# Value parts of an attention kernel: VectorE's subtraction replaced by a whole copy on ScalarE and a third step on GpSimd

## The reference

```python
edge = _attn(lin(x, n2e_q), lin(x, n2e_k), lin(x, n2e_v), adj.transpose(0, 2, 1))
edge = _ln(edge + x, norm1_g, norm1_b)
node = _attn(lin(x, e2n_q), lin(edge, e2n_k), lin(edge, e2n_v), adj)
node = _ln(x + node, norm2_g, norm2_b)
h = gelu(lin(node, ffn_w1, ffn_b1))
out = _layernorm(x + _ln(node + lin(h, ffn_w2, ffn_b2), norm3_g, norm3_b))
```

## Time and profile before

| | |
|---|---|
| median of 3 runs | 2962.13 us (2961.11 to 2962.54) |
| profiled execution, its own time | 2963.18 us |
| its span, mean granted clock | 2961.0 us, 0.989 |
| PE, DVE, ACT, POOL busy | 97%, 59%, 52%, 44% |
| attention passes | about the first 1600 us |

### The profile page before, as it was taken

One profiled execution on the slowest core, in us unless ns is written; L12 is line 12 of the kernel. 1 busy time (PEld: TensorE's weight loads), 2 busy tenths in 40 slices (PEclk: granted clock), 3 DMA queues, 4 the chain that ended last, 5 costly groups with the idle time before them and its releaser, 6 DMA issues.

```text
span 2961.0 us, 55170 instructions
## 1 busy us (share of the span) xinstructions
PE 2870.9 (97%) x17920; PEld 2400.4 (81%) x17920; DVE 1761.4 (59%) x5914; ACT 1549.1 (52%) x4138; POOL 1289.6 (44%) x1227
## 2 busy tenths in 40 slices
PE   8999999999999999999979999999999999999996
PEld 7888887888788888888868888888888888888885
DVE  7888888888888888888863332233332323333334
ACT  6777777777787877887854222222222222222221
POOL 3443534344365554546512344344343334434334
PEclk9999999999999999999989999999999999999998
DMA  6544444444566666657663011111101111110111
GB/s 197 120 112 126 117 110 116 117 123 111 147 154 162 171 170 156 166 150 176 168 155 121 22 43 58 50 57 57 57 9 55 53 53 57 57 41 22 57 36 64
DMA packets 488664, 295.44 MB, mean 100 GB/s; under 512 B 279584, under 2 KB 410784, under 8 KB 488480
## 3 DMA queue, kind: packets, MB, share of 16 engines
q1 hardware_dynamic: 488480, 293.49, 37.3%
HBM read 159.21 MB, written 67.11 MB: 76 GB/s over the span
## 4 chain that ended last, share of the span: by engine, by line
PE 81%; DVE 8%; issue 5%; ACT 4%; POOL 1%; DMA 1%; DVEq 0%; SPq 0%; ACTq 0%; POOLq 0%
PE proj L871 25%; PE proj L1335 23%; PE score L1349 12%; PE proj L1349 12%; PE score L920 5%; PE att_out L855 4%; ACT att_probs L521 2%; PE att_turn L837 2%; DVE normed L698 2%; DVE att_p_lo L769 1%; ACT turned L480 1%; DVE att_q_lo L749 1%; DVE att_stats L703 1%; DVE att_k_lo L744 1%; ACT att_p_hi L528 1%
## 5 line engine op out<-in xcount | busy, mean ns | idle before, releaser
L1279 DVE TENSOR_TENSOR hidden_lo<-hidden,hidden_hi 128x512 fp32r<-128x512 f32 x256 | 201.4, 787 | 943.1 <-ACT hidden_hi L1114 943.1
L1121 ACT ACTIVATE hidden<-proj,ffn_bias 128x512 f32<-128x512 f32 x256 | 176.6, 690 | 996.7 <-PE proj L1335 996.7
L521 ACT ACTIVATE att_probs<-att_probs,att_minus_max 128x128 f32<-128x128 f32 x1024 | 397.1, 390 | 154.7 <-DVE att_minus_max L760 154.7
L101 POOL TENSOR_TENSOR pool_scratch<-pool_scratch 128x1 f32<-128x1 f32 x144 | 38.0, 264 | 703.2 <-DVE ffn_moments L1223 402.6
L769 DVE TENSOR_TENSOR att_p_lo<-att_probs,att_p_hi 128x512 f16<-128x512 f32 x256 | 231.2, 942 | 149.2 <-ACT att_p_hi L528 149.2
L760 DVE CUSTOM_DVE_ANT_0 att_probs<-score,att_mask 128x128 f32<-128x128 f32 x1024 | 226.4, 285 | 19.2 <-PE score L920 10.7
L871 PE MATMUL proj<-weight_v_hi,source_hi 128*128 128x512 f32 x512 | 215.5, 421 | 13.7 <-DVE weight_v_lo L719 11.0
L480 ACT ACTIVATE turned<-att_turn,att_shift,att_gain 128x128 f32<-128x128 f32 x512 | 192.9, 458 | 65.6 <-PE att_turn L837 65.6
L637 POOL TENSOR_TENSOR source_lo<-source_raw,source_hi 128x512 fp32r<-128x512 f32 x128 | 163.1, 1296 | 129.6 <-ACT source_hi L544 129.6
L871 PE MATMUL proj<-source_hi,weight_k_hi 128*128 128x512 f32 x512 | 203.5, 397 | 2.3 <-DVE weight_k_lo L719 2.3
L871 PE MATMUL proj<-source_lo,weight_k_hi 128*128 128x512 f32 x512 | 203.0, 396 | 0.0
(11 more groups left out here) (157 smaller groups left out, 8520.9 us busy)
## 6 DMA issues: line engine op xcount, KB each, us to landing
att_tokens<-in_x SPq DMA_DIRECT2D x128, 256.0 KB, 3.1
source_raw<-in_x_t SPq DMA_DIRECT2D x16, 1024.0 KB, 5.5
edges_t<-turned SPq DMA_DIRECT2D x64, 256.0 KB, 2.5
source_raw<-edges_t SPq DMA_DIRECT2D x16, 1024.0 KB, 5.6
att_query_raw<-in_x_t SPq DMA_DIRECT2D x16, 1024.0 KB, 6.8
nodes_t<-turned SPq DMA_DIRECT2D x64, 256.0 KB, 2.8
source_raw<-nodes_t SPq DMA_DIRECT2D x16, 1024.0 KB, 7.5
normed<-nodes SPq DMA_DIRECT2D x16, 1024.0 KB, 5.6
```

Source lines behind the costliest of these rows:

```text
L521: nc.scalar.activation(probs[:, j, :], probs[:, j, :], ACT.Exp, bias=minus_max[:, j:j + 1], scale=-1.0, accum_out=row_sum[:, side, j:j + 1 ...
L1121: nc.scalar.activation(hidden[:, c % 2, :], up_bank[c % 2][:], ACT.Gelu, bias=bias_1[:, c:c + 1]).then_inc(activated, 1)
L1279: nc.vector.tensor_tensor(hidden_lo[:, c % 2, :], hidden[:, c % 2, :], hidden_hi[:, c % 2, :].bitcast(F32), ALU.subtract).then_inc(hidden_ ...
```

## The change

`value_high` on ScalarE now copies the bank whole, in f32, into a half of `v_rest`, after a wait that the value parts of two graphs before are done. `value_rest` on VectorE is gone. `value_low` on GpSimd casts the high part from it, subtracts it in place, casts the middle part and subtracts for the low part, with a wait between each step and the next. Value banks are now released by ScalarE, key and query banks still by VectorE, so the waits of `project` name one of two semaphores.

```diff
         def value_high(g, parity, b):
             n = value_place(g, b)
             act.wait_ge(projected, n + 1)
-            nc.scalar.copy(v_part[parity][0][:, b, :], value_bank(g, b)[:]).then_inc(proj_hi_ready, 1)
+            wait(act, values_ready, GB * g + b - 1)
+            nc.scalar.copy(v_rest[:, b % 2, :], value_bank(g, b)[:]).then_inc(proj_hi_ready, 1)
...
         def value_low(g, parity, b):
 
-            pool_gate(pool, proj_split, value_place(g, b) + 1, pool_scratch)
-            nc.gpsimd.tensor_copy(v_part[parity][1][:, b, :], v_rest[:, b % 2, :]).then_inc(v_middle_ready, 1)
+            pool_gate(pool, proj_hi_ready, value_place(g, b) + 1, pool_scratch)
+            rest = v_rest[:, b % 2, :]
+            high, middle, low = (part[:, b, :] for part in v_part[parity])
+            nc.gpsimd.tensor_copy(high, rest).then_inc(v_high_ready, 1)
+            pool.wait_ge(v_high_ready, GB * g + b + 1)
+            nc.gpsimd.tensor_tensor(rest, rest, high, ALU.subtract).then_inc(v_rest_ready, 1)
+            pool_gate(pool, v_rest_ready, GB * g + b + 1, pool_scratch)
+            nc.gpsimd.tensor_copy(middle, rest).then_inc(v_middle_ready, 1)
             pool.wait_ge(v_middle_ready, GB * g + b + 1)
-            nc.gpsimd.tensor_tensor(v_part[parity][2][:, b, :], v_rest[:, b % 2, :], v_part[parity][1][:, b, :],
-                                    ALU.subtract).then_inc(values_ready, 1)
+            nc.gpsimd.tensor_tensor(low, rest, middle, ALU.subtract).then_inc(values_ready, 1)
...
-        def value_rest(g, parity, b):
-            dve.wait_ge(proj_hi_ready, value_place(g, b) + 1)
-
-            wait(dve, values_ready, GB * g + b - 1)
-            nc.vector.tensor_tensor(v_rest[:, b % 2, :], value_bank(g, b)[:], v_part[parity][0][:, b, :],
-                                    ALU.subtract).then_inc(proj_split, 1)
-
...
-        def project(place, bank, products, chunks=range(C)):
+        def project(bank_free, bank, products, chunks=range(C)):
 
             if chunks[0] == 0:
 
-                wait(pe, proj_split, place - PROJ_BANKS + 1)
+                wait(pe, *bank_free)
...
+            if b == 2 and starts(g):
+                bank_free = (proj_hi_ready, value_place(0, 0) + 1)
+            elif b >= 2:
+                bank_free = (proj_split, split_count(g, b - 2, 1) - 2)
+            else:
+                bank_free = (proj_split, 0 if starts(g) else split_count(g - 1, b + 2, 1) - 2)
...
```

More of the change, by code:

```diff
@@ L67, in skipped, with split_count @@
     return 1 if isinstance(g, int) and g == 2 * NG - 1 and u == C - 1 else 0
+def split_count(g, u, queries):
+    return 2 * C * g + 2 * u + queries + 1
 def value_place(g, b):
@@ L320, in attention_passes @@
     projected, proj_hi_ready, proj_split = sem("projected"), sem("proj_hi_ready"), sem("proj_split")
+    v_high_ready, v_rest_ready = sem("v_high_ready"), sem("v_rest_ready")
     v_middle_ready, values_ready = sem("v_middle_ready"), sem("values_ready")
@@ L790, in body @@
                 first = starts(g) and u == 0
[L791 to L794, removed]
+                if not first:
                     mask_and_maximum(n, g if u == 1 else None)
@@ L800, in body @@
                     nc.vector.tensor_scalar(mask[:], adj[:], 0.0, MASKED, ALU.is_le, ALU.mult).then_inc(mask_ready, 1)
[L801 to L806, removed]
                 if u == 2 and not starts(g):
@@ L883, in values @@
                     pe.wait_ge(weight_lo, 3 * C * own + c + 1)
-                project(value_place(g, b), value_bank(g, b), lambda c: parts([s[:, c, b * P:(b + 1) * P] for s in x],
+                project(bank_free, value_bank(g, b), lambda c: parts([s[:, c, b * P:(b + 1) * P] for s in x],
                                                                           [w[:, c, :] for w in (wh["v"], wl["v"])]), range(c, c + 1))
@@ L892, in keys @@
             x = [s[parity] for s in (source_hi, source_lo)]
-            project(key_place(g, u) + skipped(g, u), key_bank(u), lambda c: parts([w[:, c, u * P:(u + 1) * P] for w in (wh["k"], wl["k"])],
+            project((proj_hi_ready, key_place(g, u) + skipped(g, u) - PROJ_BANKS + 1), key_bank(u), lambda c: parts([w[:, c, u * P:(u + 1) * P] for w in (wh["k"], wl["k"])],
                                                                   [s[:, c, :] for s in x]))
@@ L903, in queries @@
             x = (query_hi, query_lo) if own == 1 else [s[parity] for s in (source_hi, source_lo)]
-            project(query_place(g, u) + skipped(g, u), query_bank(u), lambda c: parts([w[:, c, u * P:(u + 1) * P] for w in (wh["q"], wl["q"])],
+            project((proj_split, split_count(g, u, 0) - 2), query_bank(u), lambda c: parts([w[:, c, u * P:(u + 1) * P] for w in (wh["q"], wl["q"])],
                                                                       [s[:, c, :] for s in x]))
@@ L913, in scores @@
             if h == 0:
-                pe.wait_ge(proj_split, query_place(g, u) + 1)
+                pe.wait_ge(proj_split, split_count(g, u, 1))
             for i in range(2):
@@ L976, in attention_passes @@
         "early_tokens_stored": (tokens_out, 16 * (NG - 1)),
-        "banks_free": ((proj_split, PROJ * last_group), (masked, UNIT * C * last_group)),
+        "banks_free": ((proj_split, 2 * C * last_group), (proj_hi_ready, PROJ * last_group), (masked, UNIT * C * last_group)),
         "residual_biased": (biased, GB * last_group),
```

## The result

The changed kernel takes 3009.1 us (median of 4 runs, 3008.0 to 3012.1) where the one before takes 2962.0 (2961.1 to 2962.5): a ratio of 1.0161, with a 95% interval of 1.0148 to 1.0175. It is slower by 47 us; 38 had been forecast, and the range of 2966 to 3030 holds it. In the profiled executions the span went from 2961.0 to 3006.2 us, 45.2 more, and this is the difference to be explained.

A forecast was written before the change was run, and what follows sets the result against it. TensorE, busy for 97% of the span, was taken to bound the kernel. Waits at the weighing, less score waits won back, plus 3.4 us of clock, came to 37.7 us on 2962.1: 3000 us (+1.3%), range 2966 to 3030.

The forecast's parts named there:

- wait at the weighing, added: TensorE's weighing in both passes: waits longer for GpSimd's value parts, 43.7 us more in all.
- wait at the scores: TensorE's scores: first pass's waits for low queries at loop returns go, 10.9 us off, 1.5 left.
- half clock: TensorE's granted clock: slow stretches behind long waits cost 10.2 us in place of 6.8, so 3.4 more.
- The longer chain: GpSimd's value part in the third unit: 4.7 us, between 4.0 and 5.2; ordinary first-pass groups wait 0.9 us each.
- the sign of an error: Weighing's wait below 10 us in total, from an f32 subtraction much cheaper than 1.2 us or an earlier inverse spread.
- First pass, behind a return: Five loop returns: weighing waits 1.9 us each, 9.5 in all; scores keep 5 x 0.3.
- The backlog of the second pass: GpSimd behind the query split: inverse spread 1.3 us late, so the weighing waits 2.4 us in an ordinary group.
- The scores of the second pass: Score waits at the second pass's loop returns: 2.7 us stay, as GpSimd is busy with a backlog.
- The clock: Half of twelve long second-pass waits followed by half clock, 6 x 1.7 = 10.2 us, in place of four now, 6.8.
- Slow clock throughout: Rival: half clock behind all the long waits, 3015 to 3034 us; chance 0.27, shared with a held ScalarE.
- Relief wins: Rival: GpSimd's chain ends before the weighing needs it, score waits go: 2937 to 2955 us; chance 0.12.
- ScalarE held by the buffer: Rival: late GpSimd stalls ScalarE's copy and the softmax, 3040 us and up; inside the slow tail, shared chance 0.27.

The follow-up runs named there:

- run 3: Kernel before, with the new way in both passes for three value parts of each group, not the one in front of the weighing: 2963.4 us, 1.0006.
- run 6: Kernel before, with the new way in the first pass only, for three value parts of four, not the one in front of the weighing: 2948.7 us, 0.9957.
- run 7: Changed kernel, with ScalarE also writing the high part from the bank, so GpSimd has three instructions per value part, not four: 2952.2 us, 0.9973.
- run 10: Changed kernel, with 95 more already met waits at the start of ScalarE's program: 3006.0 us, 1.0153.
- run 1: Changed kernel, but ScalarE also writes the high part and GpSimd makes only two parts, without the f32 subtraction (values sum wrongly): 2934.6 us, 0.9908.
- run 9: Changed kernel, with 31 more already met waits at the start of ScalarE's program: 3022.1 us, 1.0207.
- run 4: Changed kernel, with GpSimd making the value part in front of the weighing before the inverse spread, not behind it: 3018.2 us, 1.019.
- run 5: Changed kernel, with the second pass's load of the next queries issued behind a group's first transposes of the probabilities, not before: 3011.0 us, 1.017.
- run 11: Kernel before; first pass: ScalarE writes high part and whole value, GpSimd three steps; second: VectorE's last value subtraction ahead of third unit's maxima: 2971.3 us, 1.0033.

## Why the prediction was right, and where it was not

Side, size and first mechanism hold: the weighing waits for GpSimd in both passes, longest in the second, and the first pass's score waits are gone. But the terms of the sum met 45 us in another way than they had made 38:

| term, us | forecast | measured |
|---|---|---|
| wait at the weighing, added | 43.7 | 32.7 |
| wait at the scores | -9.4 | 0.0 |
| half clock | +3.4 | +11.9 |
| turns, key weights | 0 | -1.9 and +2.3 |

**The longer chain** was mis-sized. I took 4.7 us; the rows above run from the gate at 1244.78 to 1247.80 + 1.21 = 1249.01, 4.2 us. I had argued that the centring covers about half of the chain and holds GpSimd back. It is the other way round: GpSimd starts at 1244.78, VectorE at 1244.85, and the four centrings take 4.44 us where the earlier trace rows had 3.06, while GpSimd's instructions keep their length. Taken one by one the centrings last 0.96, 1.38, 0.96 and 1.37 us, and each ends 0.28 us behind one of GpSimd's casts or subtractions; the first two of the kernel before took 0.54 us each. That the one which issues first keeps the other out is also what the Trainium skill says (SBUF — State Buffer, "Who interferes with whom"); the trace agrees, with 1.38 us more on VectorE. I had used the rule for the wrong side. With 4.2 us the seven ordinary groups of the first pass lose no wait that the list shows, where 0.9 each, 6.3 us, had been summed. What had been named as the sign of an error, a cheaper f32 subtraction, is not the cause: it takes 1.17 to 1.23 us.

**First pass, behind a return:** 1.9 forecast, 10.0 / 5 = 2.0 measured; scores 1.5 left forecast, none measured. The 10.9 us that the prediction took off for the first pass hold the 0.7 where the passes meet. From 100 to 740 us the scores gained 10.2 and the weighing lost 10.0 - 0.9 = 9.1, so that the two waits together gained 1.1 us, without the clock.

**The backlog of the second pass** was right in kind and too small: the inverse spread is 2.0 us late, not 1.3. Two additional microseconds per value part had been counted; but a part whose cast lies beside VectorE's low probabilities is longer: the cast takes 1.08 instead of 0.61 and the gate 0.52 instead of 0.19. The two errors, chain and lateness, nearly cancel: 2.4 forecast for the wait in an ordinary group, 2.75 measured. Runs 3 and 6 show the backlog without the longer chain, with ScalarE's pause mixed in, and run 7 shows it gone.

**The scores of the second pass** were the step that failed. I left 2.7 us there as unchanged; it is 12.9, by ScalarE's pause. It delays the weighing's demand as well: 25.3 us at the weighing, against 29.6 in run 10 without the pause. That is why the waits behind a return, forecast at 0.9 + 1.3 = 2.2 each, came out at 0.3 to 1.9; in run 10 they are 1.9 to 2.0. That the total came so near is in part luck: 11 us less at the weighing stand against 9.4 more at the scores and 8.5 more of half clock.

**The clock** was under-counted, and not where it had been forecast. Six falls in the second pass in place of the four of the first had been summed, and the second pass has six, of 3.4 us each. Left out were three more in the first pass, from 322, 418 and 513 us on, and 3.4 us more in each of the two stretches where the passes meet: 5 x 3.4 / 2 = 8.5 us, the difference between 3.4 and 11.9. Which long wait is followed by one, and which isn't, I still can't say: in the first pass three of the five waits of 2.0 us are, and behind the wait of 2.75 us at 1249.28 none follows within 30 us.

**The rivals.** Slow clock throughout (3015 to 3034) did not come: 13 stretches, and some at the ends of the passes, for 27 waits (21 at the weighing and 6 at the scores). Relief wins: run 1 shows its full size, 27 us, and its condition, a chain without the added 2 us. ScalarE held by the buffer: not seen; its list has no wait for the value parts. GpSimd's busy time came at +229 for a forecast of +256, VectorE's at -53 for -88: over the whole span the centrings took 137.7 us where they had taken 103.0, and the low parts of the probabilities 210.8 where they had taken 231.2. The other 20 us are not traced to a line.

**Open:** what the pause is. The runs show that it comes with the loop's return, in the second pass's code, that it changes from nothing to 4 us when only the places of ScalarE's instructions change (runs 9, 10), that it shrinks when only GpSimd's order changes (run 4), and that the load of the queries has no part in it (run 5). That ScalarE's instructions arrive late is my reading. The packets of the instruction queue, which land 1.2 to 1.4 us before the end of each pause, speak for it; that they hold ScalarE's instructions, and why they come late, no run shows. Part of run 11's time is this pause, and run 7, like run 1, is without it, so run 7's 57 us is not the price of a cast alone.

## What to carry to other kernels

Taking work from an engine with slack to another with slack is paid for at the place where the receiving engine's order meets the critical one: here 2 us on GpSimd in front of a product that TensorE awaits cost 71 to 75 us over 128 parts, more than the 27 that the relief gave. Count the idle time that the receiver has between two deadlines, with its instructions at the length they have beside the other engine, and move only the instances that fit: three value parts of four, in the first pass alone, made the kernel 0.4% faster. And a change of 10 us around a hardware loop should be looked at for `issue` pauses behind the return before its own mechanism is judged.

## What had not been expected of the hardware

- A pause of ScalarE behind a loop's return of 2.2, 4.1, 4.2 us or none, with no semaphore awaited, by the place of its instructions (kernel after, runs 9, 11 and 10). It cost up to 16 us of a kernel, run 9 against run 10. Each of 28 such pauses ended 1.2 to 1.4 us after an 8192-byte packet of the instruction queue had landed.
- The four centrings on VectorE took 4.44 us where GpSimd's chain had started 0.07 us earlier, and 3.06 us where GpSimd had a gate, a cast and a subtraction beside them.
- ScalarE's copy of a 128x512 bank to f32 took 588 ns, that to bf16 590; GpSimd's subtraction of that size took 1191 ns in f32 and 1189 with bf16 written.
